# Attention values 256 columns wide, softmax sums and row maxima moved by DMA, output product over two full groups of rows, reciprocals of 128x16

## The reference, cut to what matters

```python
qkv = (x @ qkv_w.T).reshape(B, N, 3, HEADS, HEAD_DIM)       # HEADS 16, HEAD_DIM 16
attn = einsum('bhnd,bhmd->bhnm', q, k) * HEAD_DIM ** (-0.5)
attn = where(mask == 0, -inf, attn)                          # a key mask
p = softmax(attn, axis=-1)
out = einsum('bhnm,bhmd->bhnd', p, v).transpose(0, 2, 1, 3).reshape(B, N, C)
x = x + out @ proj_w.T + proj_b
x = x + mlp(adaln(x))
```

## Time and profile before

| | us |
|---|---|
| median of 3 runs | 3424.69 (3422.14 to 3424.83) |
| profiled execution | 3422.29 |
| its span | 3420.5 |
| TensorE busy (x22946) | 3288.1 (96%) |
| VectorE busy (x2916) | 2976.2 (87%) |
| ScalarE busy (x4709) | 2902.5 (85%) |
| GpSimd busy (x1087) | 2307.0 (67%) |

### The profile page before, as it was taken

The page is one execution under the profiler, slowest core; times in us unless marked ns, Lnnn a source line. Parts: engine busy times, 40 slices in busy tenths (PEclk is TensorE's granted clock), DMA queues, the critical chain, the costliest instruction groups (busy, mean ns, idle before and its releaser), DMA issues.

```text
span 3420.5 us, 59919 instructions
## 1 busy us (share of the span) xinstructions
PE 3288.1 (96%) x22946; PEld 2545.0 (74%) x22946; DVE 2976.2 (87%) x2916; ACT 2902.5 (85%) x4709; POOL 2307.0 (67%) x1087
## 2 busy tenths in 40 slices
PE   8899999999999999999999999999899989999999
PEld 5888998899989889988998899898785332222344
DVE  4998999999999999999999999999995688888231
ACT  6999999999999999999999999999893347777520
POOL 1788999999999989999998999898684000000000
PEclk8999999999999999999999999999999989999999
DMA  3222222222221222222222122222121331220000
GB/s 116 66 86 75 80 70 72 64 69 72 71 90 66 72 69 76 71 72 65 76 71 70 64 70 72 64 75 87 50 69 27 95 72 23 34 38 1 1 7 19
DMA packets 193185, 214.21 MB, mean 63 GB/s; under 512 B 75617, under 2 KB 144993, under 8 KB 192641
## 3 DMA queue, kind: packets, MB, share of 16 engines
q1 hardware_dynamic: 192898, 210.36, 21.3%
HBM read 192.19 MB, written 18.06 MB: 61 GB/s over the span
## 4 chain that ended last, share of the span: by engine, by line
PE 67%; ACT 17%; DVE 10%; issue 4%; POOL 1%; DMA 0%; SPq 0%; DVEq 0%; ACTq 0%; POOLq 0%
PE psum L1556 17%; PE psum L1331 16%; PE psum L1550 13%; PE psum L1547 10%; ACT arena L987 7%; ACT arena L970 6%; DVE arena L1235 6%; PE psum L1643 3%; PE psum L1632 3%; PE psum L1607 2%; DVE row_max L1284 2%; PE psum L1576 1%; ACT L987 1%; DVE skip_w L1310 1%; PE psum L1616 0%
## 5 line engine op out<-in xcount | busy, mean ns | idle before, releaser
L744 POOL TENSOR_TENSOR arena<-arena 128x1024 f32<-128x1024 f32 x1024 | 2237.8, 2196 | 324.7 <-DVE arena L1235 300.1
L1235 DVE TENSOR_TENSOR_SCAN arena<-arena,psum 128x512 f32<-128x512 f32 x2048 | 2371.9, 1230 | 81.6 <-PE psum L1550 49.3
L987 ACT ACTIVATE arena<-arena,a_neg 128x512 f32<-128x512 f32 x2048 | 1424.1, 712 | 45.7 <-PE psum L1550 44.1
L1556 PE MATMUL psum<-ident,arena 128*128 128x128 f32 x8192 | 1236.6, 274 | 4.7 <-POOL arena L744 4.7
L970 ACT ACTIVATE arena<-arena,bT 128x512 f32<-128x512 f32 x1536 | 1093.0, 712 | 0.0
L1550 PE MATMUL psum<-ident,arena 128*128 128x128 f32 x6144 | 1013.2, 274 | 0.0
L1556 PEld LDWEIGHTS psum<-ident,arena 128*128 128x128 f32 x8192 | 964.9, 142 | 8.0 <-POOL arena L744 7.5
L1547 PE MATMUL psum<-arena 128*128 128x128 f32 x4096 | 825.1, 284 | 59.3 <-DVE arena L1235 39.7
L1547 PEld LDWEIGHTS psum<-arena 128*128 128x128 f32 x4096 | 651.8, 192 | 276.1 <-issue 151.0
L1550 PEld LDWEIGHTS psum<-ident,arena 128*128 128x128 f32 x6144 | 747.5, 143 | 0.0
L1331 PE MATMUL psum<-arena 128*128 128x512 f32 x1472 | 706.0, 602 | 12.3 <-issue 5.0
(11 more groups left out here) (120 smaller groups left out, 1086.6 us busy)
## 6 DMA issues: line engine op xcount, KB each, us to landing
arena<-bc_dram SPq DMA_DIRECT2D x256, 512.0 KB, 3.7
arena<-diag_dram SPq DMA_DIRECT2D x224, 128.0 KB, 2.1
arena<-qk_dram SPq DMA_DIRECT2D x96, 128.0 KB
diag_dram<-arena SPq DMA_DIRECT2D x32, 256.0 KB, 4.3
qk_dram<-arena SPq DMA_DIRECT2D x12, 512.0 KB, 4.9
arena<-in_x SPq DMA_DIRECT2D x4, 512.0 KB, 10.4
arena<-in_up_w SPq DMA_DIRECT2D x1, 2048.0 KB, 11.4
out_xT<-arena SPq DMA_DIRECT2D x8, 256.0 KB, 2.3
```

Source lines behind the costliest of these rows:

```text
L744: pool.tensor_tensor(out[:, :, way], h_now[:, :, way], c_row, ALU.mult)\
L987: act.activation(decay[:, w % AHEAD, f], dt_[:, u % 2, f], ACT.Exp, scale=a_neg[:, d, f, st:st + 1])\
L1235: dve.tensor_tensor_scan(hs[:, w % RING, f, rows][:, way], decay[:, w % AHEAD, f, way], psum[:, 4 + n % U_BANKS, way], end_state(w - DS, f ...
L1556: return pe.matmul(psum[:, c, f * P:(f + 1) * P], hs[:, w % RING, f, at:at + P], ident[:, :], is_transpose=True, start=False, stop=w % DS ...
```

## The change

- v is a product of 256 columns (`v_w` without padding). ScalarE copies its 16 columns per head, and GpSimd sets columns 16 to 31 of each head to one (`ones_of_v`, before on VectorE and for one column). Every head's sum now stands in rows 16 to 31.
- `max_rows` and `copy_max_rows` are replaced by one small transposing matmul for a whole unit (`turn_top`, 96x128), one copy (`copy_top`) and three DMAs that ScalarE issues itself. For unit 0 this is a tile in LATE, and for the others it stands at step 10 of each odd block.
- `sums` and `copy_sums` are gone. SyncE (`normalise`) moves one row of sums per head to a 128x16 tile by four DMAs, VectorE inverts it in one instruction at step 8, SyncE stores it to DRAM, waits, and reads it back spread over the rows of each head. Four more DMAs pack the outputs themselves into `attnT`, two head groups to 128 rows. `attn_sb` now has two buffers.
- GpSimd multiplies only once per two units and half, and `proj` runs over two groups of rows. In END `proj 3` moves behind the eighth `up` tile.
- SyncE's order: stacks 0 to 2 are loaded first, then `normalise(v)` alternates with the loads of stacks 3 to 7. The memsets of the padding and of `sum_sel` are gone.

```diff
-        LATE += [("ones of v", 1)] + first_pass(66, SCORE_TILES + LEAD)
+        LATE += first_pass(66, 72) + [("top",)] + first_pass(72, SCORE_TILES + LEAD)
         END = [("proj", 0), ("proj", 1)] + steps("square sum std", "rms1", 0) + [("proj", 2)]\
-            + steps("recip scale", "rms1", 0) + steps("square sum std", "rms1", 1) + [("proj", 3)]\
+            + steps("recip scale", "rms1", 0) + steps("square sum std", "rms1", 1)\
             + up("rms1", 0, 0, 4) + steps("recip scale", "rms1", 1)\
-            + up("rms1", 0, 4, 8) + steps("square sum std recip scale", "rms1", 2) + up("rms1", 0, 8, 12)\
+            + up("rms1", 0, 4, 8) + [("proj", 3)] + steps("square sum std recip scale", "rms1", 2) + up("rms1", 0, 8, 12)\
...
+            def normalise(v):
+                u, qh = divmod(v, HALVES)
+                b, hg = divmod(u, HG)
+                at = hg % 2 * 4 * HD
+                sp.wait_ge(s["attn_copied"], v + 1)
+                for j in range(4):
+                    src = attn_sb[32 * j + HD:32 * j + HD + 1, v % 2].rearrange("p (k t) -> p k t", k=32)
+                    sp.dma_start(head_sums[32 * j:32 * j + 32, v % 2], src).then_inc(s[f"sums_in_{qh}"], 16)
+                for j in range(4):
+                    rows = slice(at + j * HD, at + (j + 1) * HD)
+                    sp.dma_start(attnT[b][rows, hg // 2, tok(qh)], attn_sb[32 * j:32 * j + HD, v % 2])\
+                      .then_inc(s[f"attn_in_{qh}"], 16)
+                sp.wait_ge(s["recip_ready"], v + 1)
+                sp.dma_start(sums_dram[v], head_sums[:, v % 2]).then_inc(s["sums_out"], 16)
+                sp.wait_ge(s["sums_out"], 16 * (v + 1))
+                for j in range(4):
+                    rows = slice(at + j * HD, at + (j + 1) * HD)
+                    src = sums_dram[v, 32 * j:32 * j + 32].rearrange("k t -> (k t)")
+                    sp.dma_start(recip_rows[b][rows, hg // 2, tok(qh)], src.partition_broadcast(HD))\
+                      .then_inc(s[f"attn_in_{qh}"], 16)
+            store_parts(0)
+            for u in range(STACKS):
+                load_stack(u)
+            for v in range(BLOCKS):
+                normalise(v)
+                if v % 2 == 0 and v // 2 + STACKS < B * HG:
+                    load_stack(v // 2 + STACKS)
...
+            def copy_top(u):
+                if u == 0:
+                    g = first["top",]
+                    act.wait_ge(s["tile_full"], g + 1)
+                    src = bank(g)
+                else:
+                    act.wait_ge(s["top_full"], u)
+                    act.wait_ge(s["rows_in"], 16 * PARTS * u)
+                    src = side_bank("top", u)
+                act.activation(top_rows[0:PARTS * 32], src[0:PARTS * 32, 0:P], ACT.Copy).then_inc(s["top_copied"], 1)
+                act.wait_ge(s["top_copied"], u + 1)
+                for a in range(PARTS):
+                    dst = stack[u % STACKS][ONE_ROW + 1 + a:ONE_ROW + 2 + a, 0].rearrange("p j (q t) -> p (j q) t", t=P)
+                    act.dma_start(dst, top_rows[32 * a:32 * a + 32]).then_inc(s["rows_in"], 16)
...
             def copy_attn(v):
                 act.wait_ge(s["pv_done"], (v + 1) * QT)
-                if v:
-                    act.wait_ge(s["attn_ready"], v)
-                act.activation(attn_sb[:, 0], psum[:, 4], ACT.Copy).then_inc(s["attn_copied"], 1)
+                if v >= 2:
+                    act.wait_ge(s[f"attn_in_{v % 2}"], 16 * 8 * (v // 2))
+                act.activation(attn_sb[:, v % 2], psum[:, 4], ACT.Copy).then_inc(s["attn_copied"], 1)
...
-            def reciprocals(v, k):
-                dve.wait_ge(s["sums_copied"], v + 1)
-                part = attn_sb[:, 1, k * HALF // 4:(k + 1) * HALF // 4]
+            def reciprocal(v):
+                dve.wait_ge(s[f"sums_in_{v % 2}"], 16 * 4 * (v // 2 + 1))
+                part = head_sums[:, v % 2]
                 dve.reciprocal(part, part).then_inc(s["recip_ready"], 1)
...
+            def turn_top(u, dst):
+                pe.wait_ge(s["top_ready"], 4 * (u + 1))
+                return pe.matmul(dst[0:PARTS * 32, 0:P], top_parts.rearrange("p a j q -> p (a j q)"), ident_b[:, :],
+                                 start=True, stop=True)
             def proj(q):
                 b, half = divmod(q, HALVES)
-                pe.wait_ge(s["attn_ready"], (b * HG + HG - 1) * HALVES + half + 1)
+                pe.wait_ge(s["attn_ready"], (b * HG // 2 + HG // 2 - 1) * HALVES + half + 1)
...
             def scores2(v, m):
...
-                if m < 2:
-                    pe.wait_ge(s[f"rows_ready_{qh}"], 4 * (u + 1))
+                if m == 0 and qh == 0:
+                    pe.wait_ge(s["rows_in"], 16 * PARTS * (u + 1))
```

More of the change, by code:

```diff
@@ L352, in build @@
             + steps("recip scale", "rms0", 2) + steps("square", "rms0", 3) + v_steps(0, 0, 3)\
-            + steps("sum std recip scale", "rms0", 3) + v_steps(0, 3, QT) + [("ones of v", 0)] + first_pass(0, 8)
+            + steps("sum std recip scale", "rms0", 3) + v_steps(0, 3, QT) + first_pass(0, 8)
         for n, m in enumerate(QK_ORDER):
@@ L466, in scores_at, with top_at @@
             return range(min(w, ALL_SCORES), min(w + 2, ALL_SCORES))
[L468 to L476, removed]
+        def top_at(v, m):
+            u = (v + 1) // 2
+            return u if m == TOP_STEP and v % 2 and u < B * HG else None
         for v in range(BLOCKS):
@@ L480, in build @@
                     side_tile("scores", w)
-                if m == SUMS_STEP and v:
-                    side_tile("sums", v - 1)
-                if rows_at(v, m):
-                    half, u, j = rows_at(v, m)
-                    side_tile(f"rows_{half}", 4 * u + j)
-        side_tile("sums", BLOCKS - 1)
+                if top_at(v, m):
+                    side_tile("top", top_at(v, m))
         def side_bank(kind, i):
@@ L652, in _ @@
                 load(qk_w[:, k], kp(t["qkv_w"][:, k * DM:(k + 1) * DM], 0), "attn_w_in")
[L653 to L659 removed]
+            load(v_w, kp(t["qkv_w"][:, 2 * DM:3 * DM], 0), "attn_w_in")
+            load(proj_w, kp(t["proj_w"], 0), "attn_w_in")
             def store_parts(b):
@@ L666, in store_parts, with load_stack @@
                           .then_inc(s["qk_out"], 16)
-            store_parts(0)
-            for u in range(B * HG):
+            def load_stack(u):
                 b, hg = divmod(u, HG)
@@ L756, in _ @@
                                     (STACK_AT[2], "qk_out", 16 * 2 * PARTS * B)):
+                if at == STACK_AT[2]:
+                    for b in range(B):
+                        ones_of_v(b)
+                    pool.wait_ge(s["v_ready"], B)
                 pool.wait_ge(s[name], count)
@@ L1318, in _ @@
                             finish_max(w // SCORE_TILES)
-                    if m in RECIP_STEPS and v:
-                        reciprocals(v - 1, RECIP_STEPS.index(m))
-            for k in range(4):
-                reciprocals(BLOCKS - 1, k)
+                    if m == RECIP_STEP and v:
+                        reciprocal(v - 1)
+            reciprocal(BLOCKS - 1)
             do(END)
@@ L1523, in tile @@
                     yield from v_tile(*at)
+                if kind == "top":
+                    turn_top(0, take(pe, first["top",])).then_inc(s["tile_full"], 1)
                 if kind == "proj":
@@ L1609, in scores @@
                   .then_inc(s["scores_full"], 1)
-            def max_rows(half, u, j):
-                pe.wait_ge(s["top_ready"], 4 * (u + 1))
-                dst = take_side(pe, f"rows_{half}", 4 * u + j)
-                for r in range(4):
-                    o = pe.matmul(dst[ONE_ROW:ROWS, r * P:(r + 1) * P],
-                                  top_parts[:, half * 4 + r, j, :], ident_b[:, :], start=True, stop=True)
-                o.then_inc(s[f"rows_full_{half}"], 1)
             def scores2(v, m):
@@ L1645, in weigh_v @@
                 o.then_inc(s["pv_done"], 1)
-            def sums(v):
-                pe.wait_ge(s["attn_copied"], v + 1)
-                pe.matmul(take_side(pe, "sums", v), sum_sel[:, :], attn_sb[:, 0], start=True, stop=True)\
-                  .then_inc(s["sums_full"], 1)
             do(LATE)
@@ L1657, in _ @@
             pe.wait_ge(s["scores_free"], ALONE)
-            for j in range(4):
-                max_rows(0, 0, j)
             for v in range(BLOCKS):
```

142 lines of the change are left out of this document (61 added, 81 removed).

## The result

The changed kernel takes 3381.32 us (median of 4 runs, 3380.03 to 3382.03) against 3424.76 (4 runs, 3422.14 to 3426.70) of the kernel before on the same chip: ratio 0.9875, 95% interval 0.9864 to 0.9887. It is faster by 43.4 us, 7 us less than I forecast. Its profiled execution took 3381.32 with a span of 3379.5, so the two profiled executions differ by 41.0.

A forecast was written before the change was run, and what follows sets the result against it. TensorE was taken to bound the attention and END. Terms summing to -50.6 us from the profiled 3422.3 gave 3371.7, and with 2.4 for the runs' median 3374 (own range 3368 to 3381); full range 3360 to 3394.

The forecast's parts named there:

- the rival of 3389: Blocks with score tiles: VectorE waits for sums behind stack loads, or a pair stays above 2.88 us; 3389 us, chance 0.23.
- Matmuls are time won in blocks 1 to 12: Attention blocks 1 to 12: removing row matmuls, sums and reciprocals cuts each from 26.8 to 23.3 us; -42.2 us.
- The pause on ScalarE: Step 10 of odd blocks: copy, wait and three DMA issues stall about 1.3 us each; +7.8 us, block 13 +1.8.
- the issues cost nothing: Rival for odd blocks: ScalarE's DMA issues run beside the exp and are free; 3364.5 us, chance 0.18.
- The blocks' floor: Blocks 1 to 12: 23.3 us each without a pause, plus 0.6 us in all for the transposing matmuls.
- The sums arrive in time: Reciprocal at step 8, about 13 us into a block: sums land by 9 to 13.3, so no stall; bound 3 us.
- a sign of being wrong: VectorE, no place given: its reciprocal being ended by a DMA's landing would show the prediction wrong.
- VectorE waits for the sums: Rival for five even blocks with stack loads: sums land late, 3 us each; 3389 us, chance 0.23 shared with longer pairs.
- v tiles: Before the attention blocks: half-length passes win only beside eight of the tiles, where VectorE bounds; -3.3 us.
- END: Kernel's last stretch: first up tile at 19.1 us behind a 5.3 us gap, lower clock +2.7; together -5.7 us.
- The end of the attention and blocks 13 to 15: Last sums and their copy go, -1.8 us; blocks 13 to 15 lose row groups and sums but gain a pause, -1.8.
- The slower rival: Step 10 of seven odd blocks: ScalarE's issues take several us each, deciding from 3.0; 3447 us at 4, chance 0.05.

The follow-up runs named there:

- experiment 5: Changed kernel plus four unread 128x128 reciprocals on VectorE at steps 6, 7, 9 and 10 of each block from block 1; 3393.19 us, ratio 0.9915.
- experiment 6: Changed kernel plus sixteen small unread bf16 matmuls on TensorE in each block with score tiles, at steps 8, 10, 12 and 14; 3393.71 us, ratio 0.9914.
- experiment 9: Changed kernel plus unread four reciprocals, sixteen small matmuls and an f32 product sized like the sums' in each block; 3407.29 us, ratio 0.9954.
- experiment 2: Changed kernel with the row maxima's transfers issued by GpSimd, not ScalarE, ahead of GpSimd's multiply of the even block; 3371.08 us, ratio 0.9847.
- experiment 8: Changed kernel with VectorE's reciprocal of the sums at step 5 of a block instead of step 8; 3391.79 us, ratio 0.9908.
- experiment 7: Changed kernel with each v tile computed twice, into both halves of its bank, so it costs TensorE 512 columns again; 3379.24 us, ratio 0.9872.
- experiment 3: Changed kernel with END's norm of chunk 0 ahead of proj 2's adds and proj 3 ahead of the first up tile; 3373.42 us, ratio 0.9857.
- experiment 4: Changed kernel with only proj 3 moved back ahead of the up tiles in END; 3375.46 us, ratio 0.9862.
- experiment 11: Changed kernel with GpSimd issuing row maxima early (unit 0's ahead of its last memset), chunk 0's norm first, proj 3 before up tiles; 3359.08 us, ratio 0.9812.

## Why the prediction was right, and where it was not

The time is inside the range, 0.3 above the forecast's own range, and about halfway between 3374 and the rival of 3389, whose two conditions didn't come true: a pair takes 2.89, and VectorE didn't wait for the sums beside score tiles. So the mechanism was right and its sizes were off, most of all one.

- *Matmuls are time won in blocks 1 to 12*: right. Even blocks came to 23.44 (forecast 23.3), and experiments 5, 6 and 9 gave the time back piece by piece: 1.24 in an even block for the reciprocals, 1.45 for the row matmuls, 2.4 of 3.0 for all. The last 0.6 in an even block is open.
- *The pause on ScalarE*: the mechanism was right, the term was mis-sized, and this is the step that failed. I had 7.8 in blocks 1 to 12 and 1.8 in block 13; experiment 2 measured 13.6 for all of them (11.9 and 1.7). In the blocks 7, 9, 11 and 13 the term held: issues of 0.61 beside a copy of 0.28 (taken: 0.5 and 0.6), a pause of 2.2, and a cost of 1.2, 1.2, 1.2 and 1.7 against experiment 2 (taken: 1.3, and 1.8 for block 13). The excess lies in the blocks 1, 3 and 5, which cost 1.8, 3.6 and 3.1. Their third issue took 1.1 to 1.4, and behind the stalls of 1.83 and 1.64 us the granted clock fell, which costs some 1.8 us a time; I had put that price on the gap in END and not on this one. The rival "the issues cost nothing" didn't come true on ScalarE; on GpSimd it does, and wins 13.6 where I had given it 9.5.
- *The blocks' floor* was a little low: 282.6 for blocks 1 to 12 in experiment 2 against 280.2 (12 x 23.3 + 0.6). Even without a pause, blocks are 23.44 to 23.48, and some 23.71 to 23.75. What makes those 0.27 is open.
- *The sums arrive in time*: right. In the blocks with score tiles the reciprocal is never ended by a DMA, with 0.4 us to spare at the least. In the blocks 14 and 15 and in END it is, after 20.4, 20.1 and 17.5 us in which VectorE has nothing to do. The prediction calls that a sign of being wrong, without saying where; there it holds up nobody: no gap of TensorE in the blocks 14 and 15 ends with VectorE, and END came as forecast. The rival "VectorE waits for the sums" becomes true three steps earlier (experiment 8), at about the price that I had given it: 14 us in five blocks against 15. (The total rose by 10.5. In the profiled execution it was 7.7: blocks 1 to 12 rose by 12.0, since odd ones were 1.8 shorter, and what lies ahead of block 1 was 4.9 shorter.)
- *v tiles*: -3.3 may be right. Experiment 7 gives 1.9 up to the first scores2, and 2.7 from the first score tile to block 0's end (98.3 against 95.7). Experiments 3, 4, 5, 8 and 11 have the narrow tiles too and lie between 93.4 and 95.5 there, so the size is known to some 2 us. In the changed kernel the wait for the first pass is 4.62 long, and the tiles behind it run at the lower clock:

```profile
2765.49 1.21 PE L1639 MATMUL psum<-arena 97*128 97x512 bf16 x2 [4.62 <-DVE row_max L1309]
2766.49 1.91 PE L1356 MATMUL psum<-arena 128*128 128x256 f32 x4
...
2773.74 1.03 PE L1356 MATMUL psum<-arena 128*128 128x256 f32 x4
```

  Four passes of 256 columns take 1.91 there and 1.03 later.
- *END*: right in each part. The up tile came at 19.15 (19.1), the gap was 5.15 (5.3), the clock cost 2.0 (2.7). VectorE's reciprocal of the last sums was done at 3.8 us into END (4.5 at the latest), and GpSimd's multiply at 12.6 (13):

```profile
3185.73 0.25 DVE L1336 RECIPROCAL head_sums<-head_sums 128x16 f32<-128x16 f32 x1 [17.50 <-DMA head_sums<-skip_w]
```

```profile
3193.55 1.26 POOL L796 TENSOR_TENSOR arena<-arena 128x512 f32<-128x512 f32 x1 [18.02 <-DMA arena<-sums_dram]
```

- *The end of the attention and blocks 13 to 15* came out as written, -1.8 each. Of their parts only the pause in block 13 was tested (1.7 by experiment 2, taken: 1.8); that the others add up may be luck.
- The slower rival needed 3.0 us for one issue; the worst of 24 was 1.41. The reciprocal of 128x16 takes 0.24 (taken: 0.2).

Of the 9.6 us by which the profiled gain is smaller than the sum, 6.7 lie in blocks 1 to 12, 2.1 in the unchanged stretch, 1.6 between the first score tile and block 0's end, and END gives 0.8 back. The median missed by 7.3 only, since I had added 2.4 for a median above the profiled execution, and here the two are equal.

## What to carry to other kernels

An instruction that only starts a DMA is work of the engine that it stands on: on the engine whose results the bottleneck waits for, three of them cost a stall (here 13.6 us in all, with the clock), on an idle engine they were free, provided that nothing in front of them waits. When work is taken from the bottleneck, look at what ran beside it: half the output product was also the cover of a norm, and moving another piece of it away cost 5 us. After each stall of TensorE ask also for the granted clock behind it; it can cost as much again.

## What the runs showed of the hardware

- The clock fell behind stalls of TensorE of 1.0 to 1.8 us, in a stretch in which it is busy 96% of the time, and not always: in the changed kernel behind 1.83 and 1.64, not behind 1.54 and 1.28; in experiment 3 behind 1.65 and 1.78, not behind 1.61; in experiment 8 behind 1.33, not behind 1.73; in experiment 5 behind 1.01 in three blocks, not in three others. In block 13 it fell behind a stall of 1.48 in experiments 5, 6 and 7, and not behind the same 1.48 in the changed kernel and in experiments 3 and 4. What decides is open.
- Issues of DMAs took 0.51 to 1.41 us on ScalarE, during which it ran no exp. On GpSimd three took 1.47 to 1.65.
- Transfers of 2 KB waited up to 7.9 us behind a larger load of their own queue, and 1.7 else. Transfers of 8 KB on another queue than the busy one took 3.8 to 4.6 us while the DMA engines were full, and 1.8 to 2.0 in the blocks 7 to 13.
